# Maxima of the first and the last two images by head triples, and the first softmax scores ahead of the last group's second product there too

## The chip, the core and the metric

The kernel runs on one core of a Trainium2 chip. The metric is the device time of one execution in microseconds (us), here the median of three runs. The core has five engines with an instruction queue each: TensorE (PE; PEld is its weight load), VectorE (DVE), ScalarE (ACT), GpSimd (POOL), and SyncE (SP), which only issues DMAs here. They go in the order of their own queues and meet by semaphores alone. TensorE's granted clock is told as a share of 2.4 GHz; 0.50 is the lower of its two levels, 1.2 GHz.

## The reference

Eight images of 32x32 pixels with 96 channels, so 1024 tokens each, go through three residual blocks: a mixture of 8 experts behind a group norm (MoE A), attention with 6 heads of 16 (causal), and a mixture of 4 experts (MoE C), the latter two behind a layer norm. Both mixtures keep the two best gates of a token; all experts are computed densely.

```python
x = x + _L0_conv_ref(_gn(x), ...)            # MoE A: 8 experts, 96 -> 384 -> 96, exact gelu
t = _to_tokens(x)
t = t + _L1_attn_ref(_ln_t(t), ...)          # 6 heads, softmax(q k^T / 4) v, then the projection
t = t + _L1_ffn_ref(_ln_t(t), ...)           # MoE C: 4 experts, 96 -> 384 -> 96
```

## The kernel before

**Iterations.** The kernel is a pipeline over the images. Iteration `it` computes MoE A of image `it`, the attention of image `it` - 1 and, from iteration 2 on, MoE C of image `it` - 2. Iterations 2 to 6 are alike ("middle"). Iterations 1 and 7 have no MoE C; iteration 8 has no MoE A and does MoE C of image 5 beside the attention of the last image, 7; iteration 9 does MoE C of images 6 and 7 alone. "Handover of image n" is in this text the place in iteration n + 1 where the MoE ends and the softmax of image n begins.

**A group** is one expert on 512 tokens: a first product in three parts (`ps_u`, three matmuls each, with the operands split into high and low halves of 16 bits), two gelus on ScalarE for each part (`hid`, `hidh`), their difference on POOL (`hidl`), a second product in four **quarters** of nine matmuls (`ps_y`; six with `hidh`, three with `hidl`), and its combination with the gates on VectorE (`acc`, L1164). A group takes four **slots**. In its slots TensorE does the first product of one group, the first two quarters of the group before and the last two quarters of the one before that. In the last round no first product is left and the remaining quarters come one behind the other.

**Chores** are all other work. `schedule(it)` says in which slot of the MoEs (first phase MoE A, second phase MoE C) or behind which of the 24 softmax steps each stands, and all engines walk through the same table, each doing its own share of a chore. A chore that waits holds up whatever stands behind it on its engine.

**Maxima.** The softmax wants each query's maximum ahead of the scores. 72 `max` chores (6 heads x 12 pieces, in the order of the heads) multiply queries and keys into `ps_r` (`ps_r<-ks,qs`) and reduce them on VectorE into `mpart` (L1215), with three banks in rotation. The chore `maxima` then reduces `mpart` to `mtop` (L1221), transposes it on TensorE into the bank `ps_m` that all chores share (L836), splits it into two halves `mth`, `mtl` (L1092, L1094), and SP writes these by two DMAs as two more rows of `qs` (L536). With these rows in the operand the scores (`ps_r<-qs,ks`, `ps_u<-qs,ks`) come out with the maximum subtracted.

**Softmax.** A step n is one of 24 (head triple t, 512 queries c, 128 keys j): three scores on TensorE, three exps on ScalarE (`probs`, L1014), for the keys on the diagonal a mask on POOL (L623), and two steps later the values (`ps_y<-probs,vaug`). Steps 0 to 11 belong to the heads 0 to 2, steps 12 to 23 to the heads 3 to 5. After steps 3, 11, 15 and 23 VectorE copies the finished part into `yt` (L1235). The sums then go through DRAM (`spread_sums`) to normalise `yt` in the next iteration, ahead of `project`.

**The order at the handover.** In the middle iterations `early` is true and the scores of step 0 stand in the last round ahead of the last group's second product, with `maxima` eight slots earlier:

```python
if j == 2 and early and not up:
    soft_scores(Image(it, -1), 0)
...
early = 2 <= it < NIMG - 1
```

In iterations 1 and 7 `maxima` is the first chore of the empty second phase, behind the MoE and, on VectorE, behind the last combinations; in iteration 8 it is in slot 33 of 32 to 35, the last round, and the scores of step 0 come behind all quarters.

**The front** of the next image's attention also stands there: `ln1` (statistics on VectorE, the root on POOL), `ln1_apply` (ScalarE, eight instructions in two halves), `x1_turn` (two transposes, a copy on ScalarE, the low half on VectorE), `qk` (four projections, each with such a copy and low half) and their DMAs. `ln2`, `ln2_apply`, `x2_turn`, `logits_c`, `exp_c`, `route_c` and `gates_c` are the way to MoE C's gates.

## Time and profile before

| | us |
|---|---|
| median of three runs (1362.82 to 1364.90) | 1364.79 |
| the profiled execution | 1360.14 |
| its span, first to last instruction | 1358.2 |
| TensorE busy | 1233.0 (91%) |
| ScalarE busy | 996.6 (73%) |
| VectorE busy | 807.8 (59%) |
| GpSimd busy | 801.5 (59%) |
| mean granted clock | 0.976 |

The profile is of one execution. A busy share is that of the whole span; matmuls overlap, so a busy TensorE is not one at its peak. In the timeline a row merges instructions of a kind that follow each other; the bracket at its end says how long the engine was idle before and what it waited for. A wait for several semaphores is put down to the last.

### The profile page before, as it was taken

What the parts mean: (1) busy time and instruction counts of PE and PEld (TensorE: products, weight loads), DVE (VectorE), ACT (ScalarE), POOL (GpSimd) and SP (SyncE); (2) the same over time, 40 slices, a digit from 0 to 9 for tenths busy, and PEclk for the clock granted to TensorE, in tenths of its full rate; (3) what the DMA queues carried; (4) which work ended last, traced back from release to release, by engine and by line L of the source; (5) the groups of instructions that cost most, each with busy time, mean ns of one, the idle gap of its engine ahead of it and who ended that gap; (6) DMA issues with size and microseconds to landing.
All of it is one profiled execution on the core that took longest, in us unless ns stands there. A gap on an engine that the chain in (4) does not pass through costs nothing.

```text
span 1358.2 us, 32919 instructions
## 1 busy us (share of the span) xinstructions
PE 1233.0 (91%) x12573; PEld 718.2 (53%) x12573; DVE 807.8 (59%) x2517; ACT 996.6 (73%) x2024; POOL 801.5 (59%) x815
## 2 busy tenths in 40 slices
PE   5988879999999999999999999999999988988987
PEld 2655552566536664466635665366644652462455
DVE  4784683478716784377735776178843782582343
ACT  4968548787887878877786878867787767746775
POOL 5967552667727784477816776276834662442566
PEclk9998898999999999999999999999999998997989
DMA  6002100300021000400012000310003000300100
GB/s 123 13 1 51 22 2 25 73 1 2 13 61 38 2 2 26 84 2 2 2 51 57 2 2 14 72 26 2 2 25 72 1 2 13 73 1 14 26 8 18
DMA packets 38159, 34.77 MB, mean 26 GB/s; under 512 B 26859, under 2 KB 28780, under 8 KB 38002
## 3 DMA queue, kind: packets, MB, share of 16 engines
q1 hardware_dynamic: 21362, 26.37, 9.2%
q10 hardware_dynamic: 16640, 6.29, 1.8%
q8 instruction: 100, 1.64, 0.5%
q14 instruction: 57, 0.47, 0.1%
HBM read 22.62 MB, written 9.63 MB: 24 GB/s over the span
## 4 chain that ended last, share of the span: by engine, by line
PE 59%; DVE 15%; ACT 9%; issue 6%; POOL 4%; DMA 2%; SPq 2%; DVEq 2%; POOLq 1%; ACTq 1%
PE ps_y L683 22%; PE ps_u L683 19%; PE ps_r L683 10%; PE ps_m L683 7%; POOL hidl L661 4%; DVE mpart L1215 3%; ACT hidh L975 3%; DVE acc L1164 3%; ACT xn L989 2%; DVE yt L1348 2%; ACT hid L974 2%; PE ps_m L702 1%; POOLq L641 1%; SPq L545 1%; ACT probs L1014 1%
## 5 line engine op out<-in xcount | busy, mean ns | idle before, releaser
L661 POOL TENSOR_TENSOR hidl<-hid,hidh 128x512 f16<-128x512 f32 x576 | 682.2, 1200 | 246.0 <-ACT hidh L975 238.4
L974 ACT ACTIVATE hid<-ps_u 128x512 f32<-128x512 f32 x576 | 344.9, 599 | 256.0 <-PE ps_u L683 246.4
L683 PEld LDWEIGHTS ps_y<-w2s,hidh 128*128 128x128 f16 x4608 | 276.7, 98 | 143.9 <-issue 7.9
L975 ACT ACTIVATE hidh<-ps_u 128x512 f16<-128x512 f32 x576 | 343.1, 596 | 0.0
L1215 DVE TENSOR_REDUCE mpart<-ps_r 128x1 f32<-128x512 f32 (+2 forms) x576 | 296.8, 549 | 73.4 <-PE ps_r L683 64.8
L683 PE MATMUL ps_y<-w2s,hidh 128*128 128x96 f16 x4608 | 323.7, 207 | 0.8 <-DVE acc L1164 0.8
L683 PE MATMUL ps_y<-w2s,hidl 128*128 128x96 f16 x2304 | 226.2, 208 | 3.2 <-POOL hidl L661 2.4
L623 POOL TENSOR_SCALAR_AFFINE_SELECT probs<-probs 128x384 f32<-128x384 f32 x128 | 66.6, 521 | 258.6 <-ACT probs L1014 258.4
L683 PE MATMUL ps_r<-ks,qs 96*128 96x512 f16 (+2 forms) x576 | 181.9, 329 | 19.3 <-DVE mpart L1215 13.2
L683 PE MATMUL ps_y<-probs,vaug 128*32 128x512 f32 (+3 forms) x1152 | 165.3, 510 | 1.4 <-issue 0.8
L1014 ACT ACTIVATE probs<-ps_r 128x512 f32<-128x512 f32 (+3 forms) x352 | 153.1, 511 | 18.0 <-PE ps_r L683 17.7
L683 PE MATMUL ps_u<-xah,w1h 97*128 97x512 f16 x360 | 139.2, 387 | 25.4 <-ACT hidh L975 24.3
L683 PEld LDWEIGHTS ps_y<-w2s,hidl 128*128 128x128 f16 x2304 | 142.1, 99 | 4.9 <-POOL hidl L661 4.8
L683 PE MATMUL ps_u<-xal,w1h 97*128 97x512 f16 x360 | 138.2, 384 | 0.0
L683 PE MATMUL ps_u<-xah,w1l 97*128 97x512 f16 x360 | 138.1, 384 | 0.0
L1014 ACT ACTIVATE probs<-ps_u 128x512 f32<-128x512 f32 (+3 forms) x224 | 104.3, 521 | 22.5 <-PE ps_u L683 14.5
L1164 DVE SCALAR_TENSOR_TENSOR acc<-ps_y,gatesa,acc 128x96 f32<-128x96 f32 x448 | 110.2, 308 | 6.9 <-PE ps_y L683 3.4
L683 PE MATMUL ps_r<-qs,ks 98*128 98x512 f16 (+3 forms) x352 | 94.4, 342 | 12.9 <-DMA qs<-mtl 9.3
L683 PE MATMUL ps_u<-xch,w1h 97*128 97x512 f16 x216 | 84.0, 389 | 14.4 <-ACT hidh L975 14.4
L683 PE MATMUL ps_r<-mask_q,identb 128*128 128x128 bf16 x384 | 84.2, 220 | 0.0
L683 PE MATMUL ps_u<-xch,w1l 97*128 97x512 f16 x216 | 83.4, 386 | 0.0
L683 PE MATMUL ps_u<-xcl,w1h 97*128 97x512 f16 x216 | 83.4, 386 | 0.0
(187 smaller groups left out, 1420.3 us busy)
## 6 DMA issues: line engine op xcount, KB each, us to landing
rb<-rsum_dram SPq DMA_DIRECT2D x24, 256.0 KB, 4.3
qs<-qk_dram SPq DMA_DIRECT2D x48, 96.0 KB, 3.1
ks<-qk_dram SPq DMA_DIRECT2D x48, 96.0 KB, 3.9
xin<-in_x_dram ACTq DMA_DIRECT2D x8, 384.0 KB, 3.6
qk_dram<-qk_h SPq DMA_DIRECT2D x16, 192.0 KB, 2.1
qk_dram<-qk_l SPq DMA_DIRECT2D x16, 192.0 KB, 2.3
out_dram<-xo ACTq DMA_DIRECT2D x8, 384.0 KB, 2.9
w_raw<-in_L_conv_W_dram SPq DMA_DIRECT2D x8, 288.0 KB, 5.0
```

Source lines behind the costliest of these rows:

```text
L545: sp.dma_start(sums[n:n + TT, :], yt[32 * g + HD:32 * g + HD + 1, t, :] .rearrange("a (i q) -> a i q", q=P)).then_inc(sums_in, 16)
L623: g.affine_select(out=block, in_=block, compare_op=ALU.is_ge, fill=0.0, base=0, pattern=[[0, TR], [1, P]], channel_multiplier=-1).then_inc ...
L641: pool.drain()
L661: g.tensor_tensor(hidl[:, grp.k % HB, j, :], hid[:, j, :], hidh[:, grp.k % HB, j, :], ALU.subtract).then_inc(hl_ready, 1)
L683: return nc.tensor.matmul(dst, lhsT, rhs, start=start, stop=stop, skip_group_check=True)
L974: a.activation(hid[:, j, :], bank[:], ACT.Gelu, scale=1.0 / WS)
L975: a.activation(hidh[:, grp.k % HB, j, :], bank[:], ACT.Gelu, scale=1.0 / WS).then_inc(h_ready, 1)
L989: last = a.activation(dst[:, t, :], src[:, t, :], ACT.Identity, bias=shift[:, t:t + 1], scale=rstd[:, t:t + 1])
L1014: a.activation(probs[:, n % 3, g, 0:w], soft_bank(k)[:, 0:w], ACT.Exp, scale=float(HD) ** -0.5).then_inc(p_ready, 1)
L1164: last = v.scalar_tensor_tensor(out=out[:, t, :], in0=ps_y[grp.k % 2][:, D * i:D * (i + 1)], scalar=r.gates[:, t, e:e + 1], in1=acc[:, t, ...
L1215: v.tensor_reduce(mpart[:, h, i, part:part + 1], ps_r[k % 3][:, 0:w], AX, ALU.max).then_inc(mx_free, 1)
L1348: v.tensor_tensor(yt[:, k, :], yt[:, k, :], rb[:, k, :], ALU.mult).then_inc(yn_ready, 1)
```

## The change

- `early` is true in every iteration that has a softmax. So the scores of step 0 stand ahead of the last group's second product in iterations 1, 7 and 8 too.
- In these three, `maxima` is done in two halves, one for each head triple: at slots 47 and 64 (iteration 1), 36 and 64 (iteration 7), 18 and 32 (iteration 8, where the 72 `max` chores end at slot 31 instead of 33). Each half reduces 24 columns of `mtop`, transposes the tile, splits 24 rows and issues two DMAs. The middle iterations do both halves in one chore as before (`BOTH`), with four DMAs of half the size instead of two.
- `m_stacked` becomes a semaphore for each triple. Step 0 waits for the first, step 12 for the second.
- `ln1` goes from the gap (the second phase of iterations 1 and 7) to softmax steps 0 and 3, and what follows it in the softmax goes one to three steps later; so does the way from `ln2` in iteration 8, and in iteration 9 most of the chores from `project` on go one or two slots later.

```diff
-FRONT_LATE = [(3, "ln1_apply", 0), (4, "ln1_apply", 1), (6, "x1_turn", 0), (8, "x1_turn", 1), (10, "qk", 0),
-              (11, "qk", 1), (13, "qk", 2), (15, "qk", 3)]
+FRONT_LATE = [(0, "ln1", 0), (3, "ln1", 1), (6, "ln1_apply", 0), (7, "ln1_apply", 1), (8, "x1_turn", 0),
+              (10, "x1_turn", 1), (11, "qk", 0), (12, "qk", 1), (14, "qk", 2), (16, "qk", 3)]
...
+BOTH = 2
...
-                       *maxima_at(27, SLOTS_A - 1, 0, MAXU), *GN),
-                placed((0, "maxima", 0), (1, "ln1", 0), (1, "ln1", 1)), SOFT_LATE)
+                       *maxima_at(27, SLOTS_A - 1, 0, MAXU), *GN, (47, "maxima", 0),
+                       (64, "maxima", 1)),
+                placed(), SOFT_LATE)
...
-            def stack_maxima(b):
-                wait(sp, m_split, b.value(1, 1))
+            def stack_maxima(t, b):
+                wait(sp, m_split, b.value(2, t + 1))
+                rows = slice(32 * t, 32 * t + TR * TT)
                 for n, part in enumerate((mth, mtl)):
-                    sp.dma_start(qs[MROW + n:MROW + n + 1, :, :].rearrange("a h (i q) -> a (h i) q", q=P),
-                                 part[:]).then_inc(m_stacked, 16)
+                    sp.dma_start(qs[MROW + n:MROW + n + 1, TR * t:TR * (t + 1), :]
+                                 .rearrange("a h (i q) -> a (h i) q", q=P), part[rows, :]).then_inc(m_stacked[t], 16)
...
-            def maxima_turn(b):
-                pe.wait_ge(mtop_ready, b.value(1, 1))
+            def maxima_turn(t, b):
+                pe.wait_ge(mtop_ready, b.value(2, min(t + 1, 2)))
...
                     if n == 0 and g == 0:
-                        pe.wait_ge(m_stacked, b.value(32, 32))
+                        pe.wait_ge(m_stacked[0], b.value(32, 32))
                         pe.wait_ge(mx_free, b.value(MAXU, MAXU))
+                    if k == half:
+                        pe.wait_ge(m_stacked[1], b.value(32, 32))
...
-                early = 2 <= it < NIMG - 1
+                early = attend
...
-            def maxima(b):
+            def maxima(t, b):
                 dve.drain()
-                used = mtop[:, 0:H * TT]
-                v.tensor_reduce(used.rearrange("p (h i) -> p h i", h=H), mpart[:], AX, ALU.max).then_inc(mtop_ready, 1)
-                wait(dve, m_stacked, b.value(32, 0))
+                n = TR * TT
+                some, rows = (slice(0, 2), slice(0, 32 + n)) if t == BOTH else (slice(t, t + 1), slice(32 * t, 32 * t + n))
+                done = some.stop - some.start
+                v.tensor_reduce(mtop[:, 0:64].rearrange("p (t x) -> p t x", t=2)[:, some, 0:n],
+                                mpart[:].rearrange("p (t h) i a -> p t (h i) a", t=2)[:, some], AX, ALU.max
+                                ).then_inc(mtop_ready, done)
+                for u in range(some.start, some.stop):
+                    wait(dve, m_stacked[u], b.value(32, 0))
                 shared()
-                split(mth[:], mtl[:], ps_m[0:H * TT, 0:P], -1.0 / MS).then_inc(m_free, 1)
-                dve.drain().then_inc(m_split, 1)
+                split(mth[rows, :], mtl[rows, :], ps_m[rows, 0:P], -1.0 / MS).then_inc(m_free, 1)
+                dve.drain().then_inc(m_split, done)
```

**Handover of image 0, TensorE.** In front of these rows stand, before and after, the last `max` matmuls. `ps_y0` is the older group, `ps_y1` the last one. Before, from the last quarter of all on:

```order
L683 MATMUL ps_y1<-w2s,hidh 128x96 x6
L683 MATMUL ps_y1<-w2s,hidl 128x96 x3
L836 MATMUL ps_m<-ident,mtop 128x128
L683 MATMUL ps_r0<-qs,ks 128x512
L683 MATMUL ps_r1<-qs,ks 128x512
L683 MATMUL ps_r2<-qs,ks 128x512
L683 MATMUL ps_u0<-qs,ks 128x384
```

After, from the older group's last quarter but one on; behind these rows come the other three quarters of `ps_y1` and then `ps_u0<-qs,ks`:

```order
L688 MATMUL ps_y0<-w2s,hidh 128x96 x6
L688 MATMUL ps_y0<-w2s,hidl 128x96 x3
L841 MATMUL ps_m<-ident,mtop 128x128
L688 MATMUL ps_y0<-w2s,hidh 128x96 x6
L688 MATMUL ps_y0<-w2s,hidl 128x96 x3
L688 MATMUL ps_r0<-qs,ks 128x512
L688 MATMUL ps_r1<-qs,ks 128x512
L688 MATMUL ps_r2<-qs,ks 128x512
L688 MATMUL ps_y1<-w2s,hidh 128x96 x6
L688 MATMUL ps_y1<-w2s,hidl 128x96 x3
```

The transpose has moved ahead by five quarters, the scores of step 0 by four.

**The same place, VectorE.** Before, from the last reductions to `mpart` on (`acc` and `x` are the last two combinations, `st` and `mv` the statistics of `ln1`):

```order
L1215 TENSOR_REDUCE mpart<-ps_r 128x1 x4
L1164 SCALAR_TENSOR_TENSOR acc<-ps_y,gatesa,acc 128x96 x4
L1164 SCALAR_TENSOR_TENSOR x<-ps_y,gatesa,acc 128x96 x4
L1221 TENSOR_REDUCE mtop<-mpart 128x48
L1092 TENSOR_SCALAR mth<-ps_m 48x128
L1094 SCALAR_TENSOR_TENSOR mtl<-ps_m,mth 48x128
L1194 BN_STATS st<-x 128x6 x4
```

After:

```order
L1222 TENSOR_REDUCE mpart<-ps_r 128x1 x4
L1230 TENSOR_REDUCE mtop<-mpart 128x24
L1099 TENSOR_SCALAR mth<-ps_m 24x128
L1101 SCALAR_TENSOR_TENSOR mtl<-ps_m,mth 24x128
L1171 SCALAR_TENSOR_TENSOR acc<-ps_y,gatesa,acc 128x96 x4
L1171 SCALAR_TENSOR_TENSOR x<-ps_y,gatesa,acc 128x96 x4
L1201 BN_STATS st<-x 128x6 x4
L1204 BN_AGGR mv<-st 128x2 x4
L1314 TENSOR_SCALAR xt<-xt,gmean,grstd 96x1024
```

The maxima of the second triple stand ahead of both combinations, and the group norm's application (`xt`) between the two halves of `ln1`.

**Iteration 9, TensorE.** Around the first project (`ps_m<-wp,yt`), before:

```order
L683 MATMUL ps_u<-xch,w1h 128x512
L683 MATMUL ps_u<-xch,w1l 128x512
L683 MATMUL ps_u<-xcl,w1h 128x512
L683 MATMUL ps_y<-w2s,hidh 128x96 x6
L683 MATMUL ps_y<-w2s,hidl 128x96 x3
L683 MATMUL ps_m<-wp,yt 128x96 x8
L683 MATMUL ps_u<-xch,w1h 128x512
```

After:

```order
L688 MATMUL ps_y<-w2s,hidl 128x96 x3
L688 MATMUL ps_m<-wp,yt 128x96 x8
L688 MATMUL ps_y<-w2s,hidh 128x96 x6
L688 MATMUL ps_y<-w2s,hidl 128x96 x3
L688 MATMUL ps_u<-xch,w1h 128x512
```

The project stood in slot 16, the first of its group's four; now it stands in slot 18, the third, with the quarters of slot 19 behind it.

## Rows read from the trace of the kernel before

**Rows 1.** Waits by engine, whole span: us in total, times, longest us.

```profile
PEld ps_r L683 <- DMA qs<-mtl: 9.9, 3, 3.8
```

**Rows 2.** Timeline, handover of image 0: start us, us, engine, line, operation, out<-in.

```profile
192.42 2.34 DVE L1215 TENSOR_REDUCE mpart<-ps_r 128x1 f32<-128x512 f32 x4
...
193.82 0.42 PE L683 MATMUL ps_y<-w2s,hidh 128*128 128x96 f16 x6
...
195.61 0.29 PE L683 MATMUL ps_y<-w2s,hidl 128*128 128x96 f16 x3
...
197.33 0.33 PE L836 MATMUL ps_m<-ident,mtop 128*128 128x128 f32 x1 [1.43 <-DVE mtop L1221]
...
198.42 0.63 SPq L536 DMA_DIRECT2D qs<-mth  x1
...
201.23 1.46 PE L683 MATMUL ps_r<-qs,ks 98*128 98x512 f16 x3 [3.57 <-DMA qs<-mtl]
...
202.48 0.85 PE L683 MATMUL ps_u<-qs,ks 98*128 98x384 f16 x2
...
213.81 0.69 DVE L1235 COPY yt<-ps_y 96x512 f32<-96x512 f32 x1 [3.38 <-PE ps_y L683]
...
230.99 0.68 DVE L1235 COPY yt<-ps_y 96x512 f32<-96x512 f32 x1
```

**Rows 3.** Timeline, the middle handover of image 1.

```profile
363.17 0.81 PE L683 MATMUL ps_r<-qs,ks 98*128 98x512 f16 x3
...
363.82 0.42 PE L683 MATMUL ps_y<-w2s,hidh 128*128 128x96 f16 x6
...
365.67 0.49 PE L683 MATMUL ps_u<-qs,ks 98*128 98x384 f16 x2
...
375.58 0.68 DVE L1235 COPY yt<-ps_y 96x512 f32<-96x512 f32 x1
...
387.60 0.68 DVE L1235 COPY yt<-ps_y 96x512 f32<-96x512 f32 x1
```

**Rows 4.** Timeline, handover of image 6.

```profile
1116.41 1.74 DVE L1215 TENSOR_REDUCE mpart<-ps_r 128x1 f32<-128x384 f32 x3
...
1125.34 1.28 ACT L1014 ACT_TABLE_LOAD   x1 [8.70 <-PE ps_r L683]
...
1125.90 0.85 PE L683 MATMUL ps_u<-qs,ks 98*128 98x384 f16 x2
...
1134.75 0.69 DVE L1235 COPY yt<-ps_y 96x512 f32<-96x512 f32 x1 [10.22 <-PE ps_y L683]
```

**Rows 5.** Timeline, handover of image 7.

```profile
1218.32 4.66 DVE L1215 TENSOR_REDUCE mpart<-ps_r 128x1 f32<-128x512 f32 x9
...
1223.38 0.33 PE L836 MATMUL ps_m<-ident,mtop 128*128 128x128 f32 x1 [1.55 <-DVE mtop L1221]
...
1229.80 0.85 PE L683 MATMUL ps_u<-qs,ks 98*128 98x384 f16 x2
...
1239.55 0.69 DVE L1235 COPY yt<-ps_y 96x512 f32<-96x512 f32 x1 [9.70 <-PE ps_y L683]
```

**Rows 6.** Busy us of each engine by window, then granted clock, DMA share, GB/s.

```profile
198.00:214.00 16.00, 11.97 (x68) 3.56 (x69) 7.82 (x48) 9.44 (x26) 5.14 (x8) 0.57 0.01 3
1124.00:1132.00 8.00, 6.66 (x24) 1.61 (x24) 0.45 (x5) 5.63 (x14) 3.87 (x8) 0.57 0.01 2
1224.00:1240.00 16.00, 13.22 (x74) 4.72 (x72) 4.93 (x27) 8.16 (x20) 4.16 (x8) 0.58 0.11 28
1096.00:1100.00 4.00, 1.42 (x16) 0.86 (x14) 3.63 (x13) 0.26 (x1) 1.17 (x2) 1.00 0.00 0
```

**Rows 7.** Timeline of the last iteration.

```profile
1287.72 2.92 PE L683 MATMUL ps_m<-wp,yt 96*128 96x96 f32 x16 [2.85 <-DVE yt L1348]
...
1302.87 1.55 ACT L989 ACTIVATE xn<-x,shift,rstd 128x96 f32<-128x96 f32 x4 [1.72 <-POOL shift L642]
...
1326.26 0.47 PE L716 MATMUL ps_m<-ident,gatesc 128*128 128x128 f32 x1 [3.51 <-DVE gatesc L1150]
```

44 lines of the change are left out of this document (23 added, 21 removed).

## The prediction

> **What bounds the kernel now.** I read the waits of TensorE first (the view of who waited for whom). Over the span of 1358.2 us it shows three waits of 9.9 us in total in which the softmax scores wait for the DMA that brings the maxima into `qs` [rows 1]. Three, though there are eight images: five images do it without a wait. So I took the timeline at the end of the MoE of images 0, 6 and 7 (the handovers to the softmax), and beside them that of a middle image, which already works in the order that the change gives to the three.
>
> At the handover of image 0 [rows 2] VectorE is done with the last maxima at 192.42 + 2.34 = 194.76, but it then combines two groups, so the transpose of the maxima starts only at 197.33, after 1.43 us of idle TensorE; the split, the two DMA issues and the landing take another 3.57 us, and the first scores start at 201.23. The last quarter of the second product ended at about 195.74 (its three `hidl` matmuls start at 195.61); from 193.82 on that is five quarters, so one is 0.38 us. The scores of step 1 start at 202.48, and the first copy into `yt`, the end of step 3's values, at 213.81. In the middle image [rows 3] the scores of step 0 take 363.82 - 363.17 = 0.65 us, lie ahead of the last four quarters, and step 1 follows at 365.67 with nothing idle. From step 1 to that copy it takes 375.58 - 365.67 = 9.91 us; at image 0 it takes 11.33.
>
> Image 6 [rows 4] repeats image 0, with one addition: ScalarE loads the table for exp only when the first scores are there (1125.34, 1.28 us), and step 1 starts at 1125.90. At image 7 [rows 5] the transpose stands ahead of the last quarters already; it waits 1.55 us for VectorE, and step 1 starts at 1229.80. After each of these pauses the granted clock is at its lower level, 1.2 of 2.4 GHz: its mean is 0.57, 0.57 and 0.58 over the 16, 8 and 16 us behind them [rows 6].
>
> In the last iteration (two second MoEs, no softmax) TensorE waits 2.85 us at 1287.72 for the normalised `yt` and 3.51 us at 1326.26 for the gates of image 7 [rows 7].
>
> **The change, part by part.** The sum is made against the profiled execution, 1360.14 us, with a span of 1358.2. The median of the runs is 1364.79, so 4.65 is added again at the end.
>
> 1. Handover of image 0. After the change the transpose of the second half of the maxima stands behind one quarter of the older group (ends 193.82), and VectorE makes these maxima ahead of the two combinations. Reductions end 194.76, plus 0.31 for the reduction to `mtop` (it starts at 197.02 now, its transpose at 197.33): transpose at 195.07, a wait of 1.2 us; then 0.17 of the array, one quarter 0.38, scores 0.65, four quarters 1.54: step 1 at 197.81 instead of 202.48, **4.7 us** earlier. The scores need only the first head triple's maxima, whose DMAs left 17 slots earlier; the second triple's are wanted at step 12, so their 2 us of flight hide behind twelve steps. From step 1 to the copy I take the middle image's 9.91 instead of 11.33 (the middle one has two turns there of about 0.5 us each, image 0 the logits, some 0.7): **1.4 us** more. Sum 6.1.
> 2. Handover of image 6, in the same way: reductions end at 1116.41 + 1.74 = 1118.15, transpose 1118.46, then 0.17 + 0.38 + 0.65 + 1.54: step 1 at 1121.2 instead of 1125.90, **4.7 us**. The table load moves under the four quarters, as it does in the middle. From there to the copy it took 1134.75 - 1125.90 = 8.85, which is the middle's 9.91 less its two turns: nothing more to win.
> 3. Handover of image 7. This stage goes at VectorE's pace: its reductions run without a pause from 1218.32 to 1222.98. The extra early maxima (a reduction of 0.25 that ends 0.06 ahead of the transpose, and what lies between the transpose and the first DMA issue, 198.42 - 197.33 at image 0: 1.4 us of VectorE, with a drain 1.5) push that end to about 1224.5, the transpose to 1224.8, and step 1 to 1227.6 at full clock or 1230.2 if the clock falls during that wait as it does now. Against 1229.80 this is +2.2 or -0.4, and up to 0.9 more until the copy at 1239.55. I take **1.5 us**, ends -0.4 and 3.1.
> 4. What the early half costs at images 0 and 6. At slots 47 and 36 TensorE issues its maxima and then waits for VectorE to finish them. The trace has no such wait in mid-stage. Nearest are 1.43 and 1.55 us for the same transpose behind other work; its floor is one reduction, 0.6 us, its ceiling three queued ones plus the final one, 2.3. I take 1.5 each, **-3.0 us** (-1.2 to -4.6). In the five middle images both halves go together, with the same three VectorE instructions and two more DMA issues on SP (0.63 for such a one, [rows 2]), in front of nothing that is wanted within four slots: nothing.
> 5. The rest of the softmax. ln1 (ln2 at image 7) leaves the gap and goes to steps 0 and 3, its application (two times 1.55 us of ScalarE, [rows 7]) from steps 3 and 4 to 6 and 7, turns and projections one step later. The next stretch, first to second copy, took 230.99 - 213.81 = 17.18 us at image 0 against 12.02 in the middle [rows 2, 3]. It gets 3.1 us of ScalarE, loses one projection of three, and that one lengthens the following stretch by some 2 us. With the middle as base 12.0 + 3.1 + 0.5 + 2 = 17.6: even. **0**, ends -3 and +3 for each image, not all the same way. The last projection comes one step later, and its DMAs with it, some 1.3 us; I count nothing for it.
> 6. The last iteration. The first project goes from slot 16 to 18. The normalised `yt` is ready at the same time, 1287.7, where the project now starts; but TensorE does two slots more before it, each a first product (the three matmuls' time of the scores, 0.65) and a quarter (0.38): 2.1 of the 2.85 us of waiting go. What follows ran at the lower clock. With full clock the second project, now at slot 20, ends about 3 us earlier with two more slots done, 5 us. Gates at slot 40 instead of 39 leave 3.51 - 1.0 of that wait, one more; the later application of ln2 may eat one. **5 us**, ends 2 and 8.
>
> Sum: 6.1 + 4.7 + 1.5 - 3.0 + 0 + 5 = 14.3. Profiled execution 1345.8; **predicted median 1364.8 - 14.3 = 1350.5 us**.
>
> On the clock, rows and rule differ. The three stretches spend 13.8 + 6.9 + 13.4 = 34 us at the lower level (length times twice what the mean lacks of 1, [rows 6]), yet image 6 takes no longer there than the middle image, and image 0 only 1.4 us longer, since ScalarE's exps set the pace. The Trainium skill (TensorE: Matmul & The Clock Gate, Terms) prices such a stretch at its time times one minus the share granted, that is half of it. By that rule 17 us would come back where I count about 2.
>
> **The rivals.**
> - The late chain takes it back. ScalarE is the pace of the wide steps 4 to 8, and exactly there the normalisation's 3.1 us now stand. If every one of the three softmaxes loses its 3 us, 9 are gone: gain 5.3, **1359.5**. For it: image 0's second stretch is 5 us longer than the middle's already. Against: steps 3 and 4 stood on the same engine before.
> - Waits only move: the late chain as above, and in the last iteration the wait goes from the project to ln2's application, so that item 6 is nothing. 14.3 - 9 - 5 = 0.3, **1364.5**.
> - Slower. The new mid-stage waits at slots 47, 36 and 18 let the clock fall in a stage that TensorE bounds. A fall costs as many us at the lower level as behind image 0, 13.8, of which half is lost work, 6.9. All three: 20.7 against 14.3, **1371.2**. It decides from the third fall on; one fall alone gives 1357.4, two 1364.3. Against: from 1096 to 1100, in just such a stage, TensorE is busy for only 1.42 of 4 us, and the clock stays at 1.00 [rows 6].
> - Much faster. TensorE is what these three stretches wait for after all, so that their 34 us at half the clock [rows 6] hold 17 us of work at the full one, and 17 come back instead of 2: 14.3 + 15 = 29.3, **1335.5**. Image 6 speaks against it, since there the lower clock costs nothing. (This is the result that the Trainium skill's rule above would give.)
>
> **How the numbers follow.** The forecast, a gain of 9 to 20, has 0.64; the late chain 0.17; waits that only move 0.07; slower 0.05; much faster 0.07. The forecast's own range is 1345 to 1356. With the late chain, and the unknown of items 3 to 6 on the other side, the range is **1344 to 1360**. A difference under 0.2% (2.7 us) can't be told from none in a measurement of this kernel: faster 0.88, same 0.07, slower 0.05.
>
> **What would show it.** In the changed kernel: no scores that wait for the DMA from `mtl` (item 1 to 3); step 1 of the scores about 2.7 us behind the last maxima's transpose, with the exps' table load under the last quarters (2); eleven transposes of `mtop`, the three early ones with a wait of about 1.5 us each and a clock that stays at 1.00 (3, 4, the slower rival); 17 to 18 us between the first two copies into `yt` at images 0 and 6 (5; 20 would be the late chain); a wait under 1 us at the last iteration's first project, and one of some 2.5 us for the gates (6). The prediction is wrong if the early transposes wait over 3 us, or if the softmax of these images takes 3 us more from its first copy on.

## The result, and the profile after

The changed kernel takes 1345.72 us (median of four, 1344.48 to 1349.02) against 1364.85 for the kernel before (1362.82 to 1369.94). The ratio is 0.9877, 95% interval 0.9857 to 0.9897, which is 16.8 us of 1365 with 14.1 to 19.5 as its interval; it is not the quotient of the two medians (0.9860, 19.1 us). So the kernel is faster by a little over 1%, inside the predicted range of 1344 to 1360, 4.8 us below the predicted 1350.5. The profiled execution took 1346.65 us with a span of 1344.8 and a mean granted clock of 0.986; it had 1360.14, 1358.2 and 0.976 before.

No scores wait for `qs<-mtl` any more; the line of [rows 1] is gone from the waits. The handover of image 0, the answer to [rows 2], as a timeline (start us, us, engine, line, operation, out<-in, idle time before and its releaser):

```profile
140.61 0.29 DVE L1222 TENSOR_REDUCE mpart<-ps_r 128x1 f32<-128x128 f32 x1 [5.85 <-PE ps_r L688]
...
171.77 0.33 PE L841 MATMUL ps_m<-ident,mtop 128*128 128x128 f32 x1 [1.24 <-DVE mtop L1230]
...
197.95 0.33 PE L841 MATMUL ps_m<-ident,mtop 128*128 128x128 f32 x1 [1.12 <-DVE mtop L1230]
...
198.50 0.81 PE L688 MATMUL ps_r<-qs,ks 98*128 98x512 f16 x3
...
200.68 0.49 PE L688 MATMUL ps_u<-qs,ks 98*128 98x384 f16 x2
...
208.37 0.68 DVE L1247 COPY yt<-ps_y 96x512 f32<-96x512 f32 x1
```

The order is the one announced: transpose, a quarter, scores, quarters, step 1 of the scores at 200.68, 2.73 us behind the transpose. But the transpose starts at 197.95 and step 1 only 1.8 us earlier than before, and the copy comes 5.4 us earlier. So the larger part was won behind step 1: 7.69 us from there to the copy, where it had been 11.33.

At image 6 the table load lies under the quarters, at image 7 the early half stands between two projects (`ps_m<-wp,yt`):

```profile
1119.47 0.33 PE L841 MATMUL ps_m<-ident,mtop 128*128 128x128 f32 x1 [1.12 <-DVE mtop L1230]
...
1120.49 1.28 ACT L1021 ACT_TABLE_LOAD   x1 [2.88 <-PE ps_r L688]
...
1122.21 0.49 PE L688 MATMUL ps_u<-qs,ks 98*128 98x384 f16 x2
...
1128.65 0.69 DVE L1247 COPY yt<-ps_y 96x512 f32<-96x512 f32 x1 [2.70 <-PE ps_y L688]
...
1196.33 0.33 PE L841 MATMUL ps_m<-ident,mtop 128*128 128x128 f32 x1 [1.69 <-DVE mtop L1230]
...
1197.55 2.85 PE L688 MATMUL ps_m<-wp,yt 96*128 96x96 f32 x12 [0.51 <-DVE mtl L1101]
...
1223.69 0.33 PE L841 MATMUL ps_m<-ident,mtop 128*128 128x128 f32 x1 [1.13 <-DVE mtop L1230]
...
1232.85 0.69 DVE L1247 COPY yt<-ps_y 96x512 f32<-96x512 f32 x1 [2.83 <-PE ps_y L688]
```

The answers to [rows 6], busy us of each engine by window (TensorE, its weight load, VectorE, ScalarE, GpSimd), then the granted clock: full behind all three handovers, where it was 0.57 and 0.58. In the fourth row, behind the early half of image 7, it is not.

```profile
198.00:214.00 16.00, 14.54 (x141) 5.86 (x142) 10.70 (x57) 12.50 (x32) 5.20 (x8) 1.00 0.01 2
1119.00:1133.00 14.00, 12.76 (x108) 4.91 (x108) 5.79 (x29) 11.88 (x28) 4.25 (x8) 1.00 0.01 2
1224.00:1240.00 16.00, 14.72 (x121) 5.42 (x117) 5.36 (x27) 14.67 (x35) 4.25 (x8) 1.00 0.10 27
1194.20:1204.20 10.00, 7.80 (x47) 5.95 (x46) 4.58 (x13) 1.25 (x4) 1.15 (x1) 0.66 0.01 3
```

And [rows 7] after, the first project and the gates of image 7:

```profile
1280.48 2.02 PE L688 MATMUL ps_m<-wp,yt 96*128 96x96 f32 x16 [0.56 <-DVE yt L1360]
...
1315.44 0.33 PE L721 MATMUL ps_m<-ident,gatesc 128*128 128x128 f32 x1 [0.68 <-DVE gatesc L1157]
```

To compare kernels I use stretches that start and end with the same work. The first maxima of an image are its first `mpart` row on VectorE, the first copy its first `yt<-ps_y` row. The two executions, in us:

| stretch | before | after | change |
|---|---|---|---|
| start to first maxima, image 0 | 139.68 | 140.61 | +0.93 |
| first maxima to first copy, image 0 | 74.13 | 67.76 | -6.37 |
| first to fourth copy, image 0 | 33.00 | 35.35 | +2.35 |
| from there to the fourth copy of image 5 | 787.49 | 787.87 | +0.38 |
| first maxima to first copy, image 6 | 97.09 | 93.70 | -3.39 |
| first to fourth copy, image 6 | 32.61 | 33.17 | +0.56 |
| first maxima to first copy, image 7 | 68.13 | 66.98 | -1.15 |
| first to fourth copy, image 7 | 30.56 | 30.01 | -0.55 |
| from there to the end | 88.09 | 81.94 | -6.15 |

With two short stretches that did not change the sum is -13.4, the difference of the spans.

### The profile page after: what moved, and what is told of

It is laid out like the page before. It is cut to its first block, busy times and chain, and to the rows that moved or that the text cites. A ratio compares the mean times of both kernels' runs of the same rounds, so it can differ in the third digit from the quotient of the medians.

```text
span 1344.8 us, 32972 instructions
## 1 busy us (share of the span) xinstructions
PE 1226.7 (91%) x12576; PEld 717.9 (53%) x12576; DVE 810.8 (60%) x2526; ACT 997.3 (74%) x2024; POOL 802.7 (60%) x815
## 3 DMA queue, kind: packets, MB, share of 16 engines
q8 instruction: 100, 1.64, 0.5%
## 4 chain that ended last, share of the span: by engine, by line
PE 56%; DVE 16%; ACT 11%; issue 7%; POOL 4%; DVEq 2%; DMA 2%; POOLq 1%; SPq 1%; ACTq 1%
PE ps_y L688 20%; PE ps_u L688 18%; PE ps_r L688 9%; PE ps_m L688 7%; POOL hidl L666 4%; DVE mpart L1222 4%; ACT hidh L982 3%; DVE acc L1171 3%; ACT xn L996 3%; ACT hid L981 2%; DVE yt L1360 2%; PE ps_m L707 1%; ACT probs L1021 1%; POOLq L646 1%; ACT L990 1%
## 5 line engine op out<-in xcount | busy, mean ns | idle before, releaser
L688 PE MATMUL ps_y<-probs,vaug 128*32 128x512 f32 (+3 forms) x1152 | 160.8, 497 | 0.5 <-POOL probs L628 0.2
L1021 ACT ACTIVATE probs<-ps_u 128x512 f32<-128x512 f32 (+3 forms) x224 | 104.8, 521 | 19.5 <-PE ps_u L688 11.3
L688 PE MATMUL ps_r<-qs,ks 98*128 98x512 f16 (+3 forms) x352 | 91.1, 327 | 2.3 <-ACT probs L1021 1.7
```

The lines of the kernel that those rows point to most:

```text
L688: return nc.tensor.matmul(dst, lhsT, rhs, start=start, stop=stop, skip_group_check=True)
L1021: a.activation(probs[:, n % 3, g, 0:w], soft_bank(k)[:, 0:w], ACT.Exp, scale=float(HD) ** -0.5).then_inc(p_ready, 1)
```

## The experiments

All ran on one core beside the kernel before, on four chips: the last iteration, the old front and the filled waits on one; the new front with the old handover, undivided maxima and the two of GpSimd's queue on a second; slot 22 and the two built on it (reduction apart, late half at 66) on a third; the last one on a fourth. Ratios are to the kernel before, with the 95% interval, and kernels of different chips are compared by them. Where ratio and median disagree by more than a microsecond or two, both are told. Line numbers of `kernel.py` lie a few off in some of them, and long lines of the edits are cut to the part that changed. Here, for reference, is the stretch from first maxima to first copy in the profiled execution of each:

| kernel | time, us | ratio | image 0 | image 6 | image 7 |
|---|---|---|---|---|---|
| before | 1364.85 | 1 | 74.13 | 97.09 | 68.13 |
| last iteration alone | 1356.02 | 0.9951 (0.9936 to 0.9966) | 72.42 | 100.16 | 67.81 |
| before, filled waits | 1358.69 | 0.9968 (0.9948 to 0.9988) | 72.08 | 98.87 | 66.58 |
| new front and last iteration, old handover | 1355.69 | 0.9923 (0.9897 to 0.9949) | 70.80 | 99.94 | 66.84 |
| new handover and last iteration, old front | 1358.18 | 0.9987 (0.9963 to 1.0010) | 76.56 | 102.11 | 67.32 |
| changed | 1345.72 | 0.9877 (0.9857 to 0.9897) | 67.76 | 93.70 | 66.98 |
| changed, old last iteration | 1351.36 | 0.9927 (0.9907 to 0.9947) | 67.79 | 94.26 | 66.93 |
| changed, maxima undivided | 1353.10 | 0.9913 (0.9885 to 0.9941) | 71.29 | 97.44 | 66.94 |
| changed, GpSimd's ln1 late | 1347.95 | 0.9892 (0.9861 to 0.9922) | 69.60 | 92.00 | 67.06 |
| changed, GpSimd's ln1 first | 1360.73 | 0.9989 (0.9969 to 1.0010) | 75.73 | 98.75 | 69.73 |
| changed, slot 22 | 1344.92 | 0.9873 (0.9842 to 0.9904) | 67.80 | 94.32 | 65.27 |
| and reduction apart | 1336.80 | 0.9816 (0.9789 to 0.9843) | 68.06 | 92.95 | 66.34 |
| and late half at 66 | 1338.02 | 0.9827 (0.9802 to 0.9852) | 65.93 | 90.86 | 61.31 |
| and projections earlier | 1336.73 | 0.9824 (0.9796 to 0.9852) | 65.91 | 89.21 | 62.00 |

**The last iteration.** Two runs, one takes its new places out of the changed kernel, the other puts them alone into the kernel before:

```diff
 if it == NIMG + 1:
-                       (14, "normalise_y", 1), (18, "project", 0), (20, "project", 1), (21, "ln2", 0), (22, "ln2", 1),
+                       (14, "normalise_y", 1), (16, "project", 0), (18, "project", 1), (19, "ln2", 0), (20, "ln2", 1),
...
```

> The changed kernel, with the last iteration's chores in their old slots (project at 16 and 18, ln2 at 19 and 20, its application at 23 and 24, turns at 26 and 28, the gates at 39); all else as changed. Theory: the last iteration is a gain of its own. From the last copy into yt to the end of the span the changed kernel takes 1344.8 - 1262.9 = 81.9 us, the one before 1358.2 - 1270.1 = 88.1, so this one takes 88 and its time is 1345.7 + 6.2 = 1351.9 us (from 1350 on). Rival: that stage is only shorter because it is entered differently (image 7's softmax ends another way, the clock is up); then the stretch stays at 82 and the time at 1346 to 1347.

> The kernel before, with only the last iteration's chores in their new slots. Theory: the same 6.2 us, now taken from the kernel before: 1364.8 - 6.2 = 1358.6 us, the stretch from the last copy into yt to the end at about 82. A wait of under 1 us at the first project and of some 0.7 us ahead of the gates' transpose. Rival (entered differently): 1363 to 1365 and a stretch of 86 to 88. If both this one and the last show 6, the part is independent of the handovers; if their effects don't add up, they share something.

Both came out as the theory had it, the second 2.6 us under its 1358.6. From the last copy into `yt` to the end of the span they take 87.98 and 81.64 us. Against the changed kernel the first loses 0.0050 of 1365 us, 6.8; against the kernel before the second gains 0.0049, 6.7. The part is worth 6 to 7 us and independent of the handovers.

**The old front.** The changed kernel with `ln1` behind the last group, its application at steps 3 and 4, and what follows it at its old steps too, in all three images:

```diff
-FRONT_LATE = [(0, "ln1", 0), (3, "ln1", 1), (6, "ln1_apply", 0), (7, "ln1_apply", 1), (8, "x1_turn", 0),
-              (10, "x1_turn", 1), (11, "qk", 0), (12, "qk", 1), (14, "qk", 2), (16, "qk", 3)]
+FRONT_LATE = [(3, "ln1_apply", 0), (4, "ln1_apply", 1), (6, "x1_turn", 0), (8, "x1_turn", 1), (10, "qk", 0),
+              (11, "qk", 1), (13, "qk", 2), (15, "qk", 3)]
...
-                placed(), SOFT_LATE)
+                placed((1, "ln1", 0), (1, "ln1", 1)), SOFT_LATE)
```

> The changed kernel with the normalisation put back: ln1 (ln2 at image 7) behind the last group, its application at steps 3 and 4, turns and projections one step earlier; split maxima, early scores and the last iteration as changed. Theory of the prediction (item 5 is zero): the time stays within 1.5 us of 1345.7; the first stretch (first to second copy into yt) gets shorter by about as much as the next gets longer or the first copy comes later. Rival, the late chain: the new places cost, and this kernel is faster by 1 to 3 us in each of the three softmaxes, so 1337 to 1342.

Neither side had this: 1358.18 us, 12 more than the changed kernel (15 by ratio), although split maxima and early scores are in it. The timeline of its handover of image 0:

```profile
195.70 0.33 PE L842 MATMUL ps_m<-ident,mtop 128*128 128x128 f32 x1 [1.12 <-DVE mtop L1231]
...
198.43 0.49 PE L689 MATMUL ps_u<-qs,ks 98*128 98x384 f16 x2
...
206.30 1.93 PE L689 MATMUL ps_y<-probs,vaug 128*32 128x512 f32 x6 [6.67 <-issue]
...
202.28 0.20 POOL L643 TENSOR_TENSOR shift<-mv,minus 128x8 f32<-128x8 f32 x1 [7.80 <-DVEq L1207]
...
203.31 2.07 POOL L646 TENSOR_TENSOR rstd<-rstd,power 128x8 f32<-128x8 f32 x1
...
205.67 1.47 POOL L629 TENSOR_SCALAR_AFFINE_SELECT probs<-probs 128x384 f32<-128x384 f32 x3
```

Up to step 1 of the scores all goes as in the changed kernel, 2.73 us behind the transpose. Then TensorE stands still for 6.67 us ahead of the first values. The values wait for the causal mask of step 0 on GpSimd, and in GpSimd's queue `ln1`'s shift and root stand ahead of it: these wait 7.80 us for VectorE's statistics, and the mask starts at 205.67, 3.4 us behind the shift. The profile names no releaser here ("issue"), but the first of the three masks ends at 206.20, and at image 6 of the same kernel it names the mask:

```profile
1135.39 1.93 PE L689 MATMUL ps_y<-probs,vaug 128*32 128x512 f32 x6 [5.05 <-POOL probs L629]
```

In the kernel before, step 0's mask was late for the same reason, but its scores had started only at 201.23 [rows 2], so that TensorE then waited 0.80 us:

```profile
205.09 1.93 PE L683 MATMUL ps_y<-probs,vaug 128*32 128x512 f32 x6 [0.80 <-issue]
...
204.47 1.56 POOL L623 TENSOR_SCALAR_AFFINE_SELECT probs<-probs 128x384 f32<-128x384 f32 x3
```

In the changed kernel the first mask follows its exps, and `ln1`'s part comes 7 us later:

```profile
200.56 0.53 POOL L628 TENSOR_SCALAR_AFFINE_SELECT probs<-probs 128x384 f32<-128x384 f32 x1 [3.83 <-ACT probs L1021]
...
207.61 0.20 POOL L642 TENSOR_TENSOR shift<-mv,minus 128x8 f32<-128x8 f32 x1 [2.47 <-DVEq L1206]
```

**GpSimd's queue, or VectorE, or ScalarE.** That chain has three engines in it. Two kernels have VectorE's statistics at the old place and the application at the new one; they differ in GpSimd's part alone. One has it at step 3, behind the masks:

```diff
+                    if n == 3 and it in (1, NIMG - 1):
+                        chore("ln1", 1, Image(it, 0))
+                    if n == 3 and it == NIMG:
+                        chore("ln2", 1, Image(it, -2))
                     for name, k, b in chores(it, 2, n):
-                        chore(name, k, b)
+                        if not (it == NIMG and name == "ln2"):
+                            chore(name, k, b)
...
```

> The changed kernel with VectorE's statistics of ln1 (ln2 at image 7) back in their old place behind the last group (steps 0 and 1 at image 7), but GpSimd's part of it, shift and power, at step 3 behind the causal masks, and the application at steps 6 and 7 as changed. Theory (GpSimd's queue is what the move frees): as the changed kernel, within 2 us, 1344 to 1348. Rival (VectorE is what it frees): statistics of 2.1 us ahead of the rest of VectorE's work, some 2 us a softmax or more: 1350 to 1358.

The other has it directly behind the statistics:

```diff
-FRONT_LATE = [(0, "ln1", 0), (3, "ln1", 1), (6, "ln1_apply", 0), (7, "ln1_apply", 1), (8, "x1_turn", 0),
+FRONT_LATE = [(6, "ln1_apply", 0), (7, "ln1_apply", 1), (8, "x1_turn", 0),
...
-                placed(), SOFT_LATE)
+                placed((1, "ln1", 0), (1, "ln1", 1)), SOFT_LATE)
```

> As the last, but GpSimd's part directly behind VectorE's statistics, ahead of the causal mask of step 0 (at image 7 ahead of that of step 2); application at steps 6 and 7. Theory (GpSimd's queue): the values of step 0 wait for the mask as in the run with the old normalisation, first copy into yt at image 0 at about 214 and not 208; 1355 to 1359, all of the loss of that run though the application stands late. Rival (the application on ScalarE was the cause, or VectorE): as the run with GpSimd's part late.

1347.95 and 1360.73 us. The mask of step 0 on GpSimd, first with its part late, then with it first:

```profile
198.47 0.53 POOL L628 TENSOR_SCALAR_AFFINE_SELECT probs<-probs 128x384 f32<-128x384 f32 x1 [3.84 <-ACT probs L1027]
```

```profile
202.83 0.20 POOL L642 TENSOR_TENSOR shift<-mv,minus 128x8 f32<-128x8 f32 x1 [7.80 <-DVEq L1206]
...
206.21 1.47 POOL L628 TENSOR_SCALAR_AFFINE_SELECT probs<-probs 128x384 f32<-128x384 f32 x3
```

The values of step 0 start at 199.83 in the first and at 206.84 in the second. So it is GpSimd's queue that the move of `ln1` frees. Where VectorE does the statistics, and at which step ScalarE applies them, matters at most for what lies between 1345.7 and 1348, and the intervals of these two kernels overlap.

**The front alone, and the square.** The kernel before with the new front (and the new last iteration), but its old handover:

```diff
-                placed((0, "maxima", 0), (1, "ln1", 0), (1, "ln1", 1)), SOFT_LATE)
+                placed((0, "maxima", 0)), SOFT_LATE)
...
```

> The kernel before with the new places of the normalisation (ln1 to steps 0 and 3, ln2 at image 7; application, turns and projections with them) and the new last iteration; maxima undivided, first scores behind the last group, as before. With the run that kept the old normalisation and had the new handover (12 us slower than the changed kernel), and the one with the new last iteration alone, it closes a square of four. Theory that came from that run: in the old order GpSimd's chain for ln1 (5.2 us with its power) stands ahead of the causal masks of step 0, so that the probabilities wait for it; the two parts of the change only work together. Then this kernel gains the part of the masks that came late behind scores that were late too: 1 to 3 us a softmax against the last iteration alone (1356), so 1347 to 1353. Rival: the parts add up; then it has 12 less than the last iteration alone, 1344.

1355.69 us, above the theory's 1347 to 1353. The masks do come earlier: at image 0 the first copy stands 7.98 us behind step 1 of the scores, where it is 10.61 in the run with the last iteration alone. But of these 2.6 us 2.1 go again between the first and the fourth copy (35.56 against 33.46). In ratios to the kernel before, all with the new last iteration: neither part 0.9951, the front 0.9923, the handover 0.9987, both 0.9877. Times 1365 us the front alone gains 3.8, the handover alone loses 4.9, and together they gain 10.1. Some 11 us belong to neither, only to the pair: early scores are of use only if the masks are early too. (The two singles are less sure than the pair: the intervals of the handover's and of neither just touch, those of the front's and of neither overlap, and by the medians the front gains 0.3, the handover loses 2.2 and the pair gains 10.3, so that 12 belong to the pair.)

The same distance from step 1 to the first copy at image 0 also tells the masks from the clock. It is 11.33 us before (10.61 with the last iteration alone, the same order there), 9.36 with the waits filled (run below: the clock up, the masks late), 7.98 with the new front alone (the masks early, the clock down for part of it) and 7.69 in the changed kernel. So most of the 3.6 us won there come with the masks alone; the clock alone gives 2.0, and the two overlap.

**Undivided maxima.** The changed kernel with all maxima finished at the late slot:

```diff
-                       *maxima_at(27, SLOTS_A - 1, 0, MAXU), *GN, (47, "maxima", 0),
-                       (64, "maxima", 1)),
+                       *maxima_at(27, SLOTS_A - 1, 0, MAXU), *GN,
+                       (64, "maxima", BOTH)),
...
```

> The changed kernel without the split by head triples: all maxima are finished together at the late place (slots 64, 64 and 32), the early half at slots 47, 36 and 18 is gone; scores of step 0 ahead of the last quarters and everything else as changed. Theory: the split is what makes the early scores possible. Without it the first scores wait behind the transpose for the split and the DMA (3.57 us at image 0 before), of which one quarter hides 0.4: 3.2 us of idle TensorE come back in each of the three, and behind them the low clock over the last quarters and first steps. Against that the early halves' 1.2 + 1.7 + 1.7 us of waiting go. Net 1.5 to 2 us a softmax: 5 us slower than the changed kernel, 1350 to 1352. Rival: the moved normalisation does all of it, and the split pays only for itself: 1344 to 1347.

1353.10 us. By ratio the split is worth 4.9 us, the theory's 5, with intervals that overlap; by the medians it is 7.4. It doesn't come evenly: 3.5 at image 0 and 3.7 at image 6 in the table above, and nothing at image 7, 66.94 against 66.98. There the late transpose stands 1223.69 - 1165.87 = 57.8 us behind the first maxima with the split, and 52.1 without it:

```profile
1171.70 0.62 DVE L1222 TENSOR_REDUCE mpart<-ps_r 128x1 f32<-128x128 f32 x2 [0.21 <-PE ps_r L688]
...
1223.81 0.47 PE L841 MATMUL ps_m<-ident,mtop 128*128 128x128 f32 x1 [1.17 <-DVE mtop L1230]
```

The same ten microseconds of that stage (28.3 to 38.3 behind the first maxima) have a clock of 1.00 here and of 0.66 in the changed kernel, whose row stands above:

```profile
1200.00:1210.00 10.00, 9.47 (x100) 6.75 (x99) 8.74 (x23) 4.60 (x9) 4.62 (x4) 1.00 0.01 2
```

The early half makes TensorE wait 1.69 and 0.51 us, the clock goes to its lower level, and the second project runs there, from 1197.55 to 1201.3, 3.7 us where another one at full clock takes 2.02. 5.7 us are lost in the stage, as many as the early scores win behind it (14.83 us from transpose to copy here, 9.16 with the split).

**The clock.** The kernel before, with matmuls into a free bank during its waits, and the waits left:

```diff
             def maxima_turn(b):
+                late = b.it in (1, NIMG - 1)
+                if late:
+                    filler(5)
...
+                if late:
+                    filler(15)
```

> The kernel before, with matmuls that nobody reads put into its two handovers at images 0 and 6: 5 of 512 columns ahead of the transpose of the maxima and 15 behind it, into a bank that is free then. The waits for the maxima stay, TensorE is busy during them (20 x 0.213 us = 4.3 us), so that the granted clock should stay at 1.00 behind them. Theory: ScalarE's exps are the pace, the lower clock costs at most what image 0 takes longer than a middle image from step 1 to the first copy, 11.33 - 9.91 = 1.4 us, and nothing at image 6: time 1363 to 1365, that is 0 to 2 us less than the kernel before. Rival, the clock: half of the 13.8 + 6.9 us at the lower level comes back, 10 us: 1354 to 1356. If the clock falls all the same, the run tells nothing.

1358.69 us, ratio 0.9968, or 4.4 us gained with 1.6 to 7.1 as its interval: between the theory's time and the rival's. Two windows that hold both handovers whole, in the kernel before:

```profile
192.00:216.00 24.00, 17.60 (x147) 7.13 (x144) 14.63 (x72) 12.98 (x32) 6.90 (x11) 0.72 0.01 2
1120.00:1140.00 20.00, 13.54 (x65) 3.73 (x65) 4.50 (x23) 13.63 (x33) 4.29 (x8) 0.83 0.01 2
```

and with the waits filled:

```profile
192.00:216.00 24.00, 20.40 (x177) 8.95 (x174) 15.54 (x74) 13.85 (x34) 7.58 (x12) 0.93 0.01 2
1120.00:1140.00 20.00, 16.59 (x84) 5.06 (x83) 4.60 (x22) 14.27 (x34) 4.29 (x8) 0.91 0.01 1
```

Reckoned as in the prediction (length times twice what the mean lacks of 1), 20.2 us at the lower level before (13.4 and 6.8) and 7.0 with the filler; the run with the last iteration alone, whose handovers are those of the kernel before, has 0.72 and 0.74 there, 23.8 us. So 13 to 17 us at the lower level cost about 4 us here, more than my 1.4 and less than the rival's 10. The filler itself overran by half a microsecond. From the transpose to the first copy the filled kernel takes 14.42 us at image 0 and 14.07 at image 6, the kernel before 16.48 and 13.95, the run with the last iteration alone 15.76 and 15.42: 1.3 to 2.1 us at image 0, at image 6 1.4 against the one and nothing against the other. Together that is 1.9 to 2.7 us, inside the interval.

**Image 7's early half behind the projects.**

```diff
-                       (20, "keep_x1", 0), *maxima_at(2, 31, 0, MAXU), (18, "maxima", 0), (32, "maxima", 1)),
+                       (20, "keep_x1", 0), *maxima_at(2, 31, 0, MAXU), (22, "maxima", 0), (32, "maxima", 1)),
```

> The changed kernel with one number changed: the early half of image 7's maxima stands at slot 22 of that stage, behind the two projections (17 and 19), and no longer at 18 between them. Theory, from the runs so far: with the early half that stage, from its first maxima to the late transpose, takes 57.8 us, in the run with undivided maxima 52.1. Of the 5.7, 1.69 + 0.51 are waits of TensorE at slot 18 and 19; behind them the clock is at its lower level for some 6 us, in which the second projection (1.99 us at full clock) takes 3.5. Behind the projections there is less queued on VectorE, the wait is 1.7 or less with no second one directly behind it, and the clock holds: 1 to 2 us instead of 5.7, so 4 us faster than the changed kernel, 1341 to 1343. Rival: any pause of TensorE there drops the clock, or the 5.7 come from VectorE's queue: within 1.5 us of 1345.7.

1344.92 us, a ratio of 0.9873: no difference to the changed kernel can be told. The stretch to the first copy is 1.7 us shorter, not 4. The wait is as long at slot 22 (1.75 us), and the clock falls behind it there:

```profile
1204.00:1208.00 4.00, 3.70 (x26) 2.41 (x27) 1.99 (x5) 0.32 (x1) 0.23 (x1) 0.57 0.02 3
```

Only the projects no longer stand in that stretch. The wait had to go, not to be moved.

**The reduction apart.** In all three images VectorE's last reduction of the early half gets a chore of its own, a slot ahead of the transpose:

```diff
+    "top":          (-1, 0),
...
-                       *maxima_at(27, SLOTS_A - 1, 0, MAXU), *GN, (47, "maxima", 0),
+                       *maxima_at(27, SLOTS_A - 1, 0, MAXU), *GN, (47, "top", 0), (48, "maxima", 0),
...
-MAXU), (36, "maxima", 0),
+MAXU), (36, "top", 0), (37, "maxima", 0),
...
-(18, "maxima", 0), (32, "maxima", 1)
+(21, "top", 0), (22, "maxima", 0), (32, "maxima", 1)
```

> As the last, and in all three images VectorE's final reduction of the early half stands one slot ahead of the transpose (slots 47, 36 and 21, transposes at 48, 37 and 22), so that TensorE has a slot's work while VectorE gets there. Theory: the early half's cost is TensorE waiting for that reduction (1.24 and 1.71 us at images 0 and 6, and 1.84 us longer from the first maxima to the late transpose at image 0 against undivided maxima); it falls to under 0.5 each: 2 to 3 us faster than the last run, 1339 to 1341. Rival: VectorE bounds these stretches and is itself the length, so that the wait only moves to the maxima behind: no change against the last.

1336.80 us: 0.9816 against 0.9873 with slot 22 alone, and its interval ends below the changed kernel's. The three early transposes wait 0, 0.46 and 0.33 us instead of 1.24, 1.71 and 1.69:

```profile
169.82 0.33 PE L842 MATMUL ps_m<-ident,mtop 128*128 128x128 f32 x1
...
1079.20 0.33 PE L842 MATMUL ps_m<-ident,mtop 128*128 128x128 f32 x1 [0.46 <-DVE mtop L1233]
...
1203.58 0.33 PE L842 MATMUL ps_m<-ident,mtop 128*128 128x128 f32 x1 [0.33 <-DVE mtop L1233]
```

The gain, 8 us by the medians, is more than the waits of 3.9 us. Where it comes from isn't shown. The profiled execution (1341.5 us, the longest of its five) has a span 3.5 us shorter than that of slot 22 alone, 1.9 of them ahead of image 0's first maxima, where the two kernels are alike, and its stretches from first maxima to first copy are no shorter in sum (+0.3, -1.4 and +1.1 us). The last section shows two falls of the clock in it that gave back some 5 us; that the four shorter executions were spared them would explain the gain, but they have no trace.

**The late half behind the first scores.**

```diff
-                       (64, "maxima", 1)),
+                       (66, "maxima", 1)),
...
-(32, "maxima", 1)
+(34, "maxima", 1)
```

> As the last, and the late halves stand behind the first scores and the first of the last quarters (slots 66, 66 and 34 instead of 64, 64 and 32). Theory: at 64 TensorE waits 1.1 us for the second triple's maxima while two quarters lie ready, and the scores of step 0 need only the first triple's. Now it does these quarters in that wait: step 1 of the scores and the first copy into yt come 0.8 us earlier in each of the three, 2 us faster than the last run, 1337 to 1340. Rival: the scores wait for VectorE's last reductions of maxima anyway (they free the banks), and nothing moves; or the second triple's maxima come too late for step 12, which would show as a wait there.

1338.02 us, no difference by time. In the profile it does what was meant: the late transposes wait for nothing, the first copies come 2.1 us earlier at images 0 and 6 (68 to 66 and 93 to 91 in the table) and 5.0 at image 7 (where it was also spared a fall of the clock, last section), and no scores of step 12 wait. In this execution 4 us were lost again in the last iteration, whose chores are the same (84.65 us from the last copy to the end against 80.42).

**Projections earlier.** Last, the third and fourth projection of the front one step earlier:

```diff
-              (10, "x1_turn", 1), (11, "qk", 0), (12, "qk", 1), (14, "qk", 2), (16, "qk", 3)]
+              (10, "x1_turn", 1), (11, "qk", 0), (12, "qk", 1), (13, "qk", 2), (15, "qk", 3)]
```

> As the last run (early halves apart, late halves at 66), with the third and fourth projection of images 1 and 7 one step earlier in the softmax beside them (steps 13 and 15, their places of before, instead of 14 and 16). In all runs with the new places of the normalisation the stretch from the second to the third copy into yt takes 6.2 us at images 0 and 6 against 4.2 with the old ones, and the next one 0.5 less. Theory (item 5 of the prediction: the projection that one step pushes over the second copy lengthens the stretch behind it by some 2 us): the stretch from second to third copy goes back to some 4.2, the one before it gets longer by less than that, 1 us less for each of the two images, time 1336 to 1337. Rival: ScalarE's copies of the projections are the length wherever they stand; the sum of the stretches stays and the time is that of the last run, 1338.

1336.73 us, 1.3 less than the last and within its spread. The stretch from second to third copy of image 0 went from 6.22 to 5.06 us, but the one before it from 17.97 to 20.33 and the one behind from 11.15 to 11.64: 1.7 us longer in all, at image 6 0.7. The theory falls; the places of the change were the better ones for the softmax itself. These last three kernels are 1.7 to 1.8% faster than the kernel before and 0.5 to 0.6% faster than the changed one; which of them is best the runs don't tell.

## Why the prediction was right, and where it wasn't

The direction, the range and the size held: 14.3 us forecast, 13.4 in the profiled executions, 16.8 by ratio, 19.1 by the medians. Item 6 was right as reasoned. That the three handovers came out right in sum was partly luck, as the parts show:

- **Item 1 with item 4, image 0** (6.1 - 1.5 = 4.6): 6.4 measured. The order of events and the 2.7 us from transpose to step 1 were right. Counted from the first maxima, step 1 came 2.7 us earlier, where 4.7 - 1.5 = 3.2 were foretold, and the copy another 3.6 behind it, where 1.4 were. Wrong was the base for what follows. I let step 1 to the copy go from 11.33 to the middle image's 9.91, since that is a handover with early scores; it went to 7.69. And the reason that I gave for the gain, one queue (TensorE's), was not enough. I named VectorE and SP as what stands around the handover and never looked at GpSimd's queue, though `ln1` was to leave it. With the new handover and the old front, which is what item 1 reckoned with, the runs show a loss for the three images together, 4.9 us by ratio and 2.2 by the medians. The sum came out right because the change happened to contain the other half.
- **Item 2 with item 4, image 6** (3.2): 3.4. This agreement says less than it seems to. Counted from the first maxima, step 1 came only 1.0 us earlier instead of 3.2; the rest was won behind it. I had put the distance from step 1 to the copy (8.85) down as having nothing more to win; it is now 6.44. Besides, the stage ahead of it varies between executions of the same order: from the first maxima to the late transpose it takes from 82.8 to 85.8 us in the six kernels that are alike there.
- **Item 3, image 7** (1.5): 1.15, out of two errors that cancel. I added 1.4 us of VectorE's work to the stage; it became 5.9 us longer, by the wait, the clock and a project in slow motion. From the transpose to the copy I had expected 16.17 to shrink by some 3; it shrank to 9.16.
- **Item 4** (1.5 us of waiting each at images 0 and 6): 1.24 and 1.71, and 1.69 at image 7, where only VectorE's 1.4 us had been counted (item 3). The waits were right, what they cost was not everywhere. At image 0 the late transpose stands 57.34 us behind the first maxima with the early half and 55.51 without it, 1.8; at image 7 5.7.
- **Item 5** (0): +2.35, +0.56 and -0.55 us from first to fourth copy, 2.4 in all. Inside the ends, and not the late chain's 9. At image 0 the first stretch became 17.97 us long, near my 17.6. The second went from 4.18 to 6.23, and that is the projection's 2 us: I had put them into the first stretch's sum and then called that sum even, so they were never charged.
- **Item 6** (5): 6.15, and 6.8 and 6.7 in two separate runs. The first project waits 0.56 us, as said; of the wait for the gates 0.68 was left, where I had kept 2.5.

Of the rivals, **slower** (a fall of the clock at a new mid-stage wait) was real in one of three places in this execution; in that of the slot-22 run, alike at image 6, the clock fell behind image 6's early half as well (0.57 over 1081 to 1085, against 1.00 here). I had argued the fall away with a row of 4 us in which a little busy TensorE kept its clock [rows 6]. That row shows a wait for VectorE, and the changed kernel has the same wait at nearly the same time. First the kernel before, then the changed one:

```profile
1098.66 0.39 PE L683 MATMUL ps_r<-ks,qs 96*128 96x512 f16 x1 [2.58 <-DVE mpart L1215]
...
1098.00:1102.00 4.00, 3.34 (x32) 2.10 (x33) 3.79 (x13) 2.07 (x4) 1.10 (x1) 1.00 0.01 4
```

```profile
1097.99 0.39 PE L688 MATMUL ps_r<-ks,qs 96*128 96x512 f16 x1 [2.58 <-DVE mpart L1222]
...
1098.00:1102.00 4.00, 4.00 (x24) 2.27 (x25) 3.08 (x9) 1.09 (x3) 1.15 (x1) 0.57 0.01 4
```

The run with the last iteration alone, which is the kernel before up to there, has 0.60 in that window. So my row was one outcome of a pause that can also end the other way. **Much faster** was nearer than I gave it: the filler run gives back a quarter to a third of the time at the lower level. The Trainium skill (TensorE: Matmul & The Clock Gate, Terms) would price the 13 to 17 us that the filler kept out of the lower level at half, an estimate of 6.6 to 8.4 us; the run gives 4.4, with 1.6 to 7.1 as its interval, so it excludes only the upper end of that. At image 0 alone 10.0 us less at the lower level shortened the stretch by 1.3 to 2.1, where the rule, again as an estimate, would have 5. My own term for the clock, 1.4 us, lies just outside the interval.

## What to carry to other kernels

A step that leaves a gap leaves it on every engine: write down what is queued behind it on each, the one with little to do above all, before crediting the gain to the engine that waited. Here a mask behind a root on GpSimd took the whole gain.

Where one engine's result is wanted by another in the middle of a dense stage, let the producer's last step stand a slot ahead of the consumer's. Three waits of 1.2 to 1.7 us fell to under 0.5 in this way, and the kernel got 8 us faster; that the waits account for all of it is not shown.

When a total comes out right, compare the parts. Two errors of 4 us each cancelled at image 7, and the run without the split showed it.

## What the runs showed of the hardware

TensorE's clock falls behind pauses as short as one or two microseconds, and not each time. The kernel with the reduction apart and the one with its late half at 34 have the same instructions up to slot 32 of image 7's stage. Both wait 1.64 us for VectorE at the same place:

```profile
1183.65 0.28 PE L689 MATMUL ps_r<-ks,qs 96*128 96x256 f16 x1 [1.64 <-DVE mpart L1223]
```

```profile
1181.75 0.28 PE L689 MATMUL ps_r<-ks,qs 96*128 96x256 f16 x1 [1.64 <-DVE mpart L1223]
```

Behind it the first ran at 1.2 GHz, the second stayed at 2.4. The granted clock over the 4 us from 3.2 us behind that row:

```profile
1186.85:1190.85 4.00, 4.00 (x23) 3.11 (x21) 1.26 (x3) 1.09 (x2) 1.53 (x2) 0.50 0.00 0
```

```profile
1184.95:1188.95 4.00, 4.00 (x44) 3.27 (x42) 2.19 (x6) 1.14 (x3) 1.55 (x2) 1.00 0.00 0
```

Nine of the traces have this wait of 1.63 or 1.64 us, 20.8 us behind the first maxima of image 7, and in three of them the clock falls directly behind it. The project behind it took 3.69 us in the first kernel and 1.99 in the second, and the stage from first maxima to late transpose 57.18 us against 53.81. In the same way the 1.12 us ahead of image 0's late transpose cost nothing in the changed kernel (10.42 us from there to the copy) and 1.6 in the kernel with the reduction apart (12.06), where the first scores took 1.34 us instead of 0.81. Such a pause is thus a chance of 1.6 to 3.4 us more (the latter at the least, since the second kernel's late transpose stands further back in the order), and a part of the 0.3% by which its executions differ may come from there; how much, no run shows.
